# Graph attention on one Trainium2 core: an early K projection, edges and a shorter root on Pool, and another order of the last jobs

## What is computed

```python
def attention(x, adj, Wq, bq, Wk, bk, Wv, bv, beta):
    q = split_heads(x @ Wq + bq)
    k = split_heads(x @ Wk + bk)
    v = split_heads(x @ Wv + bv)
    scores = einsum('bhqd,bhkd->bhqk', q, k) / sqrt(32)
    scores = scores + beta * adj[:, None]
    scores = where(adj[:, None] > 0, scores, -9e15)
    out = einsum('bhqk,bhkd->bhqd', softmax(scores), v)
    return merge_heads(out)

x = layernorm(x + attention(x, adj, ...))      # eps 1e-5
```

## Time and profile before

| | |
|---|---|
| median of 3 runs | 625.36 us (624.7 to 625.64) |
| the profiled execution | 624.76 us, its span 622.9 us |
| PE busy | 602.4 us, 97% |
| DVE busy | 592.3 us, 95% |
| ACT busy | 576.9 us, 93% |
| POOL busy | 401.7 us, 64% |
| matmul clock granted | 0.99 of full speed on average |
| HBM | 22.94 MB read, 12.58 MB written |

### The profile page before, as it was taken

One profiled execution on the slowest core, in us unless ns is written; L12 is line 12 of the kernel. 1 busy time (PEld: TensorE's weight loads), 2 busy tenths in 40 slices (PEclk: granted clock), 3 DMA queues, 4 the chain that ended last, 5 costly groups with the idle time before them and its releaser, 6 DMA issues. The chain is left out here.

```text
span 622.9 us, 20663 instructions
## 1 busy us (share of the span) xinstructions
PE 602.4 (97%) x6080; PEld 488.5 (78%) x6080; DVE 592.3 (95%) x2266; ACT 576.9 (93%) x2063; POOL 401.7 (64%) x639
## 2 busy tenths in 40 slices
PE   7899999999999999999999999999999999999991
PEld 7887878787878888787878787888878787878850
DVE  4989999999999999999999999999999999999885
ACT  4899999999999999999999999999999999999981
POOL 1333327667767767776766776776777676677664
PEclk9999999999999999999999999999999999999996
DMA  6248889888889988888998888998888898887832
GB/s 195 85 104 193 182 170 229 187 200 203 196 202 204 223 183 202 200 202 195 223 195 197 198 201 198 205 223 182 202 203 201 196 224 189 200 202 172 191 94 102
DMA packets 56190, 117.61 MB, mean 189 GB/s; under 512 B 10512, under 2 KB 12304, under 8 KB 56080
## 3 DMA queue, kind: packets, MB, share of 16 engines
q1 hardware_dynamic: 54992, 116.10, 80.2%
q10 hardware_dynamic: 1088, 0.20, 0.2%
HBM read 22.94 MB, written 12.58 MB: 57 GB/s over the span
## 5 line engine op out<-in xcount | busy, mean ns | idle before, releaser
L521 ACT ACTIVATE probs<-neg_scores,neg_max 128x256 f32<-128x256 f32 x768 | 382.3, 503 | 5.1 <-DVE neg_max L603 1.4
L603 DVE CUSTOM_DVE_ANT_0 neg_scores<-s_bank,bias_sb 128x256 f32<-128x256 f32 x768 | 279.8, 415 | 9.8 <-PE s_bank L466 6.9
L638 DVE STREAM_TRANSPOSE blocks<-probs 128x512 f32<-128x512 f32 x308 | 196.8, 686 | 0.0
L521 ACT ACTIVATION_READ_ACCUMULATOR probs<-neg_scores,neg_max 128x1 f32 x768 | 149.5, 195 | 0.0
L847 POOL TENSOR_SCALAR adj_sb<-adj_sb,beta_col 128x512 f32<-128x512 f32 x31 | 62.2, 2008 | 81.4 <-DVE bias_sb L651 81.4
L466 PE MATMUL s_bank<-qk 32*128 32x256 f32 x1536 | 110.0, 400 | 2.4 <-DVE neg_max L603 1.8
L390 PE MATMUL j_bank<-xt_high,w_high 128*128 128x256 f32 x567 | 110.5, 303 | 0.4 <-DVE xt_low L619 0.3
L537 ACT ACTIVATE qk<-j_bank,qk_bias 128x256 f32<-128x256 f32 x192 | 90.0, 470 | 17.3 <-PE j_bank L390 15.6
L466 PEld LDWEIGHTS s_bank<-qk 32*128 32x128 f32 x1536 | 69.4, 184 | 42.5 <-ACT qk L537 13.3
L889 POOL TENSOR_SCALAR att<-att,rstd,shift 128x384 f32<-128x384 f32 x58 | 95.6, 1656 | 6.3 <-POOL shift L886 6.3
L419 PE MATMUL j_bank<-shuffled,v_sb 128*32 128x256 f32 x1232 | 98.1, 385 | 0.2 <-ACT blocks L533 0.2
(11 more groups left out here) (82 smaller groups left out, 867.3 us busy)
## 6 DMA issues: line engine op xcount, KB each, us to landing
shuffled<-blocks SPq DMA_DIRECT2D x480, 160.0 KB, 4.1
x_sb<-in_x_dram SPq DMA_DIRECT2D x32, 384.0 KB, 6.1
out_dram<-att SPq DMA_DIRECT2D x30, 384.0 KB, 3.4
adj_sb<-in_adj_dram SPq DMA_DIRECT2D x32, 256.0 KB, 6.1
shuffled<-blocks SPq DMA_DIRECT2D x16, 128.0 KB, 2.6
blocks<-in_L_gnn_Wq_dram SPq DMA_DIRECT2D x1, 576.0 KB, 5.8
blocks<-in_L_gnn_Wk_dram SPq DMA_DIRECT2D x1, 576.0 KB, 8.0
blocks<-in_L_gnn_Wv_dram SPq DMA_DIRECT2D x1, 576.0 KB, 5.3
```

The lines of the kernel that those rows point to most:

```text
L521: nc.scalar.activation(probs[:, (T * s + t) % (T * NX), :], neg_scores[:, (T * s + t) % (T * NH), :], ACT.Exp, bias=neg_max[:, n % 2, t, h ...
L603: nc.vector.tensor_tensor_reduce(neg_scores[:, (T * s + t) % (T * NH), :], s_bank[h % J][:, t * N:(t + 1) * N], bias_sb[:, n % 2, t, :], - ...
L638: nc.vector.transpose(blocks[:, n % 2, :, h, :, :].rearrange("p k t q -> p t k q"), probs[:, slot:slot + T, :].rearrange("p t (k q) -> p t ...
```

## The change

It has four parts.

1. In graph 0, K(2,0) runs at h = 0, ahead of the second scores; it ran at h = 2.
2. `edges` of the graphs 2 to 31 is done by Pool, at the head of `bias`, on its own wait for the adjacency and for the maxima that read this bias buffer last. DVE keeps those of the graphs 0 and 1.
3. Pool's root uses another form: -0.5 times the variance is kept, and each Newton round is, for each of the two columns, two instructions that take rstd as a per-partition pointer operand. The columns alternate, so an instruction waits for the one two before it.
4. In the last graph G(1,30) and O(1,31) run at h = 9, in front of the transposes of heads 10 and 11, and G(1,31) at h = 10. Graph 30's sum with x is one instruction over all columns at h = 10.

```diff
-    CHAIN = 4 * NEWTON + 2
+    CHAIN = 2 * T * NEWTON + 3
@@ jobs_of, n == 0
+                0: (("K", 2, 0),),
                 1: (("K", 0, 1),),
-                2: (("K", 2, 0), ("Q", 0, 1)),
+                2: (("Q", 0, 1),),
@@ jobs_of, last graph
-                9: (("G", 0, n - 1), ("O", 2, n - 1)),
-                10: (("G", 1, n - 1), ("O", 1, n)),
-                11: (("G", 2, n - 1),),
+                9: (("G", 0, n - 1), ("O", 2, n - 1), ("G", 1, n - 1), ("O", 1, n)),
+                10: (("G", 2, n - 1), ("G", 1, n)),
-    last_jobs = (("O", 2, B - 1), ("G", 1, B - 1), ("G", 2, B - 1))
+    last_jobs = (("O", 2, B - 1), ("G", 2, B - 1))
@@ moments_pair, i == 1
-                    sum_with_x(n, slice(2 * P, D))
-                    dve.wait_ge(part_summed, 2)
+                    dve.wait_ge(part_summed, 1)
@@ norm_last
-                take(("G", 1, B - 1))
                 sum_with_x(B - 1, slice(0, 2 * P))
                 take(("G", 2, B - 1))
                 sum_with_x(B - 1, slice(2 * P, D))
-                dve.wait_ge(part_summed, 4)
+                dve.wait_ge(part_summed, 3)
@@ DVE's loop
-                    if h == 11 and n + 2 < B:
-                        edges(n + 2)
...
                     elif n == B - 1 and h == 10:
-                        sum_with_x(B - 2, slice(0, 2 * P))
+                        sum_with_x(B - 2, slice(0, D))
@@ Pool, bias(n)
+                if n >= 2:
+                    pool.wait_ge(adj_in, (n + 1) * DMA)
+                    pool.wait_ge(max_ready, T * H * (n - 1))
+                    take_wait()
+                    nc.gpsimd.tensor_scalar(key_order(bias_sb[:, n % 2, :, :]), by_keys(adj_sb[:, :, :]), 0.0, MASKED,
+                                            ALU.is_le, ALU.mult).then_inc(not_edge_ready, 1)
@@ Pool, layer_norm(n)
-                nc.gpsimd.tensor_scalar(var_eps[:, :], mean_var[:, n % 2, :, 1], 1.0, EPS, ALU.mult, ALU.add).then_inc(var_ready, 1)
-                link(nc.gpsimd.tensor_scalar(rstd[:, :].bitcast(I32), var_eps[:, :].bitcast(I32), -0.5, float(RSQRT_SEED),
-                                             ALU.mult, ALU.add))
+                linked(link(nc.gpsimd.tensor_scalar(var_eps[:, :], mean_var[:, n % 2, :, 1], -0.5, -0.5 * EPS, ALU.mult, ALU.add)))
+                seed_at = link(nc.gpsimd.tensor_scalar(rstd[:, :].bitcast(I32), var_eps[:, :].bitcast(I32), -0.5, HALF_SEED,
+                                                       ALU.mult, ALU.add))
                 for _ in range(NEWTON):
-                    link(nc.gpsimd.tensor_tensor(nt_a[:, :], rstd[:, :], rstd[:, :], ALU.mult))
-                    link(nc.gpsimd.tensor_tensor(nt_b[:, :], nt_a[:, :], var_eps[:, :], ALU.mult))
-                    link(nc.gpsimd.tensor_scalar(nt_c[:, :], nt_b[:, :], -0.5, 1.5, ALU.mult, ALU.add))
-                    link(nc.gpsimd.tensor_tensor(rstd[:, :], rstd[:, :], nt_c[:, :], ALU.mult))
+                    for t in range(T):
+                        linked(rstd_at[t])
+                        b_at[t] = link(nc.gpsimd.tensor_scalar(nt_b[:, t:t + 1], var_eps[:, t:t + 1], rstd[:, t:t + 1],
+                                                               rstd[:, t:t + 1], ALU.mult, ALU.mult))
+                    for t in range(T):
+                        linked(b_at[t])
+                        rstd_at[t] = link(nc.gpsimd.tensor_scalar(rstd[:, t:t + 1], nt_b[:, t:t + 1], 1.5, rstd[:, t:t + 1],
+                                                                  ALU.add, ALU.mult))
```

More of the change, by code:

```diff
@@ L191, in graph_attention_program @@
         rstd = sb("rstd", [P, T])
-        nt_a = sb("nt_a", [P, T])
         nt_b = sb("nt_b", [P, T])
-        nt_c = sb("nt_c", [P, T])
         shift = sb("shift", [P, T])
@@ L238, in graph_attention_program @@
         moments_ready = sem("moments_ready")
-        var_ready = sem("var_ready")
         chain = sem("chain")
@@ L865, in layer_norm @@
             def layer_norm(n):
-                step = [0]
+                step = [CHAIN * n]
                 def link(ins):
@@ L870, in link, with linked @@
                     ins.then_inc(chain, 1)
-                    pool.wait_ge(chain, CHAIN * n + step[0])
+                    return step[0]
+                def linked(count):
+                    pool.wait_ge(chain, count)
                     take_wait()
@@ L875, in layer_norm @@
                 take_wait()
-                nc.gpsimd.tensor_scalar(var_eps[:, :], mean_var[:, n % 2, :, 1], 1.0, EPS, ALU.mult, ALU.add).then_inc(var_ready, 1)
-                pool.wait_ge(var_ready, n + 1)
-                take_wait()
-                link(nc.gpsimd.tensor_scalar(rstd[:, :].bitcast(I32), var_eps[:, :].bitcast(I32), -0.5, float(RSQRT_SEED),
-                                             ALU.mult, ALU.add))
-                for _ in range(NEWTON):
-                    link(nc.gpsimd.tensor_tensor(nt_a[:, :], rstd[:, :], rstd[:, :], ALU.mult))
-                    link(nc.gpsimd.tensor_tensor(nt_b[:, :], nt_a[:, :], var_eps[:, :], ALU.mult))
-                    link(nc.gpsimd.tensor_scalar(nt_c[:, :], nt_b[:, :], -0.5, 1.5, ALU.mult, ALU.add))
-                    link(nc.gpsimd.tensor_tensor(rstd[:, :], rstd[:, :], nt_c[:, :], ALU.mult))
-                link(nc.gpsimd.tensor_tensor(shift[:, :], mean_var[:, n % 2, :, 0], rstd[:, :], ALU.mult))
-                assert step[0] == CHAIN
+                linked(link(nc.gpsimd.tensor_scalar(var_eps[:, :], mean_var[:, n % 2, :, 1], -0.5, -0.5 * EPS, ALU.mult, ALU.add)))
+                seed_at = link(nc.gpsimd.tensor_scalar(rstd[:, :].bitcast(I32), var_eps[:, :].bitcast(I32), -0.5, HALF_SEED,
+                                                       ALU.mult, ALU.add))
+                rstd_at = [seed_at, seed_at]
+                b_at = [0, 0]
+                for _ in range(NEWTON):
+                    for t in range(T):
[6 more added lines that the diff above has]
+                                                                  ALU.add, ALU.mult))
+                linked(rstd_at[T - 1])
+                linked(link(nc.gpsimd.tensor_tensor(shift[:, :], mean_var[:, n % 2, :, 0], rstd[:, :], ALU.mult)))
+                assert step[0] == CHAIN * (n + 1)
                 for t in range(T):
```

## The result

The change makes the kernel 3.5 us faster in the first comparison: 622.12 us (median of 5 runs, 621.97 to 622.19) against 625.64 for the kernel before on the same chip (624.70 to 626.04), ratio 0.9946, 95% interval 0.9931 to 0.996. So the gain is 2.4 to 3.5 us.

A forecast was written before the change was run, and what follows sets the result against it. TensorE's own order of work was taken to bound the steady stretch, with ScalarE full in the head. 624.76 - 1.03 - 0.0 = 623.7 us for the profiled execution, the median 0.6 over it: 624.3 us, range 622.8 to 634.

The forecast's parts named there:

- Step 1: Head: K(2,0) ahead of the second scores fills TensorE's wait there; 1.03 us faster, bounds 0 and 1.27.
- Step 2: Steady stretch and head: edges leaving VectorE for 30 graphs only lengthens VectorE's idle time or is given back; 0 us.
- The forecast's own sign: Steady stretch of the changed profile: a period under 18.3 us, against 18.36, would prove step 2 wrong.
- Rival D: Steady stretch: VectorE does bound the period; 30 times 0.31 us, 9 us faster, 615 us; chance 0.06.
- Step 3: Pool, each period: edges adds 1.95 us, the short root saves 0.4; 17.8 us under 18.36, effect on the time 0.
- Rival C: Pool's root: pointer instructions cost more, so Pool becomes the bound; slower, 632 us and over in most; chance 0.17.
- Step 4: Last graph, VectorE's chain: -0.1, +1.0 idle before G(1,30), -0.9 from takes and one sum; 0.0 us, between -0.5 and +0.5.
- Rival E: Port shared by Pool and VectorE: Pool's edges holds it, up to 1.5 us a graph, 29 times, 668 us; chance 0.03.
- this trace has the lock once: Shared port: shift on Pool at 606.25 took 0.69 us instead of 0.20 while VectorE's sum ran.

The follow-up runs named there:

- edges twice: The kernel before, with edges done twice on VectorE in 30 graphs: 639.76 us against 625.29, ratio 1.0234.
- edges_later: The kernel before, with edges still on VectorE but behind the xt_low that K(1,n+1) waits for: 626.28 us, ratio 1.0022.

## Why the prediction was right and wrong

- **Step 1, K(2,0): right to the hundredth.** Forecast 1.03 us; the head is 1.03 us shorter with it alone and 1.01 to 1.04 in the whole change. That VectorE's maxima, not TensorE, would set the third scores was the term that made it 1.03 and not 1.06: after, the scores start 0.15 us behind the last row of the maxima.
- **Step 2, edges: wrong.** All of the miss came with this part of the change. The step said "TensorE's own order of work is the period ... a VectorE instruction less changes nothing there". That is the step that failed. VectorE bound the period together with TensorE, with a distance of 0.024 us between them: without edges the period is 18.347 instead of 18.371 us, and with 0.58 us more on VectorE it is 0.59 us longer. What led me there: the steps that I compared lie behind O jobs, whose inputs are long ready, and none of them holds the one place where TensorE waits for VectorE, the bank of K(1,n+1). The 0.20 us in which VectorE was not busy I read as slack, but 0.10 of it is a wait for TensorE's scores at 308.23, in the same loop of waits. And the periods that I called constant differ by 10 to 40 ns from graph to graph, which a loop of two engines does and TensorE alone would not: with edges gone they agree within 10 ns up to the hole in VectorE's program. The forecast's own sign, "a period under 18.3 us would prove step 2 wrong", was too coarse to see it: 18.347 disproves the step and does not reach that sign.
- What it cost: 1.48 us, of which VectorE's bound is 0.58, the small waits of the long stretch. The other 0.9 are no load and were in no term of the forecast: the middle hole in VectorE's program (0.31 before, 0.08 after), the hole in the last root (0.34), the step between Pool's closing semaphore instructions (0.29) and 0.05 of small change in the tail. Where such a hole falls is luck as far as these runs tell. By the bound alone the time would have been near 623.0 us (an estimate, 622.12 and 0.9), just inside the range: the failed step made the forecast too high, and luck took the time out of the range.
- In the head the step held: beside the K move edges brought nothing there (44.00 us with and without it). Alone it brought 0.17 us, and leaving it out on both engines 0.03.
- **Rival D, "VectorE does bound the period", was the true mechanism of the steady stretch, with a wrong price.** I gave it 9 us, the whole 0.31 a graph. The chance of 0.06 was for that price. Two bounds 0.024 us apart give a gain of 0.024 a graph when one is lifted, and a loss of the whole dose when it is raised, as 14.5 us for 0.58 a graph shows. The rival between, a small gain per graph times 28, had no place in my list; the lower end of the range, 622.8, left room for it alone but not for the 0.9 us beside it.
- **Step 3, Pool: right in its effect and its prices, too careful in its sum.** 2.00 for 1.95 us, 0.347 and 0.271 for 0.35 and 0.27. Rival C (a jump for having a pointer at all) was wrong. The twelve root instructions take 3.4 us from start to start (12 times 0.28) where the sum had 4.1, since the two columns overlap. So Pool has 0.6 to 0.9 us left and not 0.56. The short root is what keeps this: without it the waits before the sum with x are gone.
- **Step 4, the last graph: right.** Forecast 0.0 us, an idle microsecond made up by takes back to back; +0.05 us in the trace, and alone 0.1 us faster, inside the noise.
- **Rival E, the port: wrong for the steady stretch.** Edges on Pool and on neither engine have the same periods. The Trainium skill (Perfetto Trace Analysis, Optimizing Scalar/DVE Operations) warns that moving work between the two might not help; here it helped by as much as leaving the work out. But the prediction's "this trace has the lock once" missed a larger case, in the head, which the last section shows.
- The sum: -1.03 + 0 was forecast, -1.01 and -1.48 stand in the trace. The runs of the parts alone have -1.0 for K(2,0) and -1.3 for edges.

## What to carry to other kernels

An engine that is busy for 99% of a period bounds it until a wait is found that proves otherwise: look for the other engine's waits at every place where it can be held (each bank's release too, four jobs back), and at waits of 10 to 40 ns, not only at steps that happen to be constant. In this kernel periods that scatter by 0.2% (18.35 to 18.39 us) were the sign of two engines that wait for each other in a loop; with one engine as the bound, in the kernel after, 18 periods in a row took 18.346 or 18.347 us. Two traces laid side by side matmul by matmul name the place. The cheapest test of a supposed slack is to add work there: 0.58 us added and 0.59 us longer says more than any busy share. And before a stretch of a profile is put down to an edit, look at its granted clock and at how far this execution is from the median.

## What the chip showed that I had not expected

- Instructions of one column on Pool whose waits are already met follow each other at 0.28 us, with 347 and 271 ns each; the old chained ones of two columns at 0.38 us with 197 ns each. Two independent chains hide the 0.18 us of idle time between chained instructions.
- VectorE has holes of 0.2 to 0.35 us at a few places in 620 us that move with its program. Taking edges out took one off the last root, 0.3 us that belong to no operation.
- Groups of projections run at 113 or at 118 ns a matmul, and V jobs at 1.66 or 1.69 us, in stretches of many graphs with the same instructions; after the hole at 404 us the period of the kernel after is 18.360 instead of 18.347 with no wait that the trace shows. The kernel with K(2,0) and edges moved keeps 18.347 to the end, and that with the old last graph has 18.360 from about 240 us on. The cause stays open.
- VectorE's first edges waits for Pool. Rows of before, Pool's first sum of x and bv and VectorE's edges:

```profile
9.78 1.83 POOL L857 TENSOR_TENSOR x_sb<-x_sb,bv_row 128x768 f32<-128x768 f32 x1 [8.32 <-DMA bv_row<-in_L_gnn_bv_dram]
10.21 1.67 DVE L651 TENSOR_SCALAR bias_sb<-adj_sb 128x512 f32<-128x512 f32 x1 [1.23 <-DMA adj_sb<-in_adj_dram]
```

  In all 14 profiles this edges starts while Pool's sum runs, between 9.97 and 10.52 us, and takes 1.25 to 2.08 us instead of the 0.39 to 0.45 of the later ones; and in all 14 it ends 0.28 to 0.29 us after Pool's sum has ended. The two do not use each other's data, so VectorE is held until Pool's instruction has run, as a lock between the two would do; what is locked no run here shows. In 12 of the 14 the first maxima follow Pool's end by 4.13 to 4.20 us (4.35 and 4.36 in the other two). So Pool's start, which waits for a load, is behind most of their scatter of 0.5 us.
- The granted clock was 0.50 (1.2 GHz) for a stretch of the head in four profiles. In three of them (edges twice, the last graph alone, the last graph in its old order) the stretch lies between 8.1 and 11.9 us, ahead of the first maxima, and from there on their heads are as long as without it. In that of edges_later TensorE was in the projections at 20.6 us, and it cost 1.5 us.
